# Three rows parked in device memory, the third batch made ahead of the down products, and float32 transposes, in a fused attention and feed-forward kernel

## What is computed

```python
x = x + xattn(layernorm(x), ctx, Wq, bq, Wk, bk)     # x (4, 512, 512), ctx (4, 512, 256)
x = x + ffn(layernorm(x), gate_w, up_w, down_w)      # inner width 2048

def xattn(q_rows, feat, ...):
    query, key = feat @ Wq.T + bq, feat @ Wk.T + bk
    attention = softmax(query @ key.T, axis=-1)      # (4, 512, 512)
    return einsum('bln,bmn->blm', q_rows, attention)

def ffn(x, ...):
    gate, up = mx_linear(x, gate_w), mx_linear(x, up_w)
    return mx_linear(silu(gate) * up, down_w)
# mx_linear(x, w) = mx_dequant(x) @ mx_dequant(w).T
# mx_dequant: per 32 values a scale max|v|/448, v/scale rounded to float8 e4m3, times the scale, float32
```

## Time and profile before

| | us |
|---|---|
| median of 3 runs | 609.74 |
| lowest, highest | 608.04, 609.96 |
| span of the profiled execution | 608.0 |

### The profile page before, as it was taken

How to read it: one execution, slowest core, us unless ns; L and a number is a source line. 1 busy time by engine, 2 the same in 40 slices (tenths; PEclk the granted TensorE clock), 3 DMA queues, 4 the chain that set the end, 5 groups by cost and what they waited for, 6 DMA issues and landing times.

```text
span 608.0 us, 7215 instructions
## 1 busy us (share of the span) xinstructions
PE 600.6 (99%) x2683; PEld 282.3 (46%) x2683; DVE 484.0 (80%) x455; ACT 309.2 (51%) x463; POOL 44.8 (7%) x60
## 2 busy tenths in 40 slices
PE   8999999999999999999999999999999999999998
PEld 3456554444444444444444444444444444444446
DVE  4999998899999999988999985131148899989740
ACT  3999989553555555853475532431121515254520
POOL 0000002100000001010110201000000000001100
PEclk9999999999999999999999999999999999999999
DMA  8989869989988978867445655750010334557691
GB/s 314 396 206 275 234 177 256 280 193 249 208 207 209 219 159 210 174 140 171 124 112 97 148 112 113 165 86 0 1 19 0 53 69 83 90 105 101 110 171 35
DMA packets 148162, 92.28 MB, mean 152 GB/s; under 512 B 134304, under 2 KB 134688, under 8 KB 143264
## 3 DMA queue, kind: packets, MB, share of 16 engines
q1 hardware_dynamic: 142656, 63.78, 45.2%
q0 software_dynamic: 5472, 28.05, 19.9%
HBM read 25.76 MB, written 8.39 MB: 56 GB/s over the span
## 4 chain that ended last, share of the span: by engine, by line
PE 85%; DMA 5%; issue 3%; ACT 3%; DVE 1%; SPq 1%; POOL 0%; DVEq 0%; ACTq 0%
PE bank L727 49%; PE bank L739 17%; PE bank L742 9%; PE bank L711 5%; DMA h<-in_ctxT 2%; PE bank L702 1%; PE bank L695 1%; DMA xT<-hT 1%; PE bank L687 1%; PE bank L757 1%; DMA W<-hT 1%; DMA h<-hT 1%; ACT hT L944 1%; PE bank L762 1%; ACT h L987 0%
## 5 line engine op out<-in xcount | busy, mean ns | idle before, releaser
L727 PE MATMUL bank<-gu_hi,xT 128*128 128x512 f16 x1024 | 243.6, 380 | 1.7 <-DMA xT<-hT 1.7
L727 PEld LDWEIGHTS bank<-gu_hi,xT 128*128 128x128 f16 x1024 | 99.9, 98 | 123.4 <-DMA xT<-hT 3.2
L727 PE MATMUL bank<-gu_lo,xT 128*128 128x512 f16 x512 | 131.5, 379 | 0.0
L739 PE MATMUL bank<-dn,hT 128*128 128x512 f16 x480 | 106.1, 379 | 0.0
L1633 DVE SCALAR_TENSOR_TENSOR h<-bank,unscale,silu 128x512 f32<-128x512 f32 x64 | 47.4, 747 | 56.1 <-PE bank L727 36.1
L1088 ACT ACTIVATE silu<-bank,unscale 128x512 f32<-128x512 f32 x64 | 42.8, 679 | 83.4 <-PE bank L727 40.3
L727 PEld LDWEIGHTS bank<-gu_lo,xT 128*128 128x128 f16 x512 | 50.1, 98 | 60.4
L739 PEld LDWEIGHTS bank<-dn,hT 128*128 128x128 f16 x480 | 47.0, 98 | 56.6
L1114 ACT ACTIVATE W<-h 128x2048 f16<-128x2048 f32 x16 | 30.5, 1909 | 68.3 <-DVE W L1665 25.4
L711 PE MATMUL bank<-dn,h 128*128 128x512 f32 x128 | 55.9, 593 | 0.0
L742 PE MATMUL bank<-dn,hT 128*128 128x512 f16 x240 | 54.3, 379 | 0.0
(11 more groups left out here) (119 smaller groups left out, 560.1 us busy)
## 6 DMA issues: line engine op xcount, KB each, us to landing
W<-hT POOLq DMA_DIRECT2D x12, 1024.0 KB, 5.9
W<-in_units SPq DMA_DIRECT2D x11, 1024.0 KB, 5.7
h<-W POOLq DMA_DIRECT2D x7, 1024.0 KB, 6.1
h<-in_xcols SPq DMA_DIRECT2D x4, 1024.0 KB, 12.6
out_y<-y POOLq DMA_DIRECT2D x12, 256.0 KB, 6.2
h<-in_xrows SPq DMA_DIRECT2D x2, 1024.0 KB, 11.8
out_y<-h SPq DMA_DIRECT2D x2, 1024.0 KB, 5.5
h<-hT POOLq DMA_DIRECT2D x2, 1024.0 KB, 5.9
```

The costliest lines, as they stand in the source:

```text
L727: last = pe.matmul(bank[:, :], xT[:, b % 2, part, k, :], w[:, c, g, j * 512:(j + 1) * 512], start=(j == 0 and not low), stop=(j == HT - 1 ...
L739: pe.matmul(bank[:, :], hT[:, r % 2, 0, k, :], dn[:, w, k, :], start=(k == 0 and w == 0), stop=False)
```

## The change

- `turn_probs` uses `pe.transpose` with the identity, and `weigh` scales the 128x512 row of probabilities in place by 1/sum, 16 times. The diagonals go.
- The second layernorm's rows of batch 2 are centred from SBUF (`X[2]`) into a place in the `dn` tensor that is free until the units 8 to 11 come, and not read back from `out_y`. They get their own place, so they may be made early: `n2` now comes between u7 and u8. Units 8 to 11 wait until their transposes are through.
- `h` has still 7 slots, but a table of them. Rows 4, 5 and 6, once whole, are stored to `park` in device memory (`park_row`), their slots are given to rows 7, 8 and 9, and they are read back into slots 2, 3 and 2 (`bring_row`) after the low parts of rows 2, 3 and 4 are made.
- The lists are in a new order. PE makes 44 products before `down(0)`; it was 32.
- The scratch output of `row_means` and `row_variances` is `y`, and batch 3's statistics are made later.
- All the orders (products, banks, rounds, SP, POOL, ACT, DVE) are new. The number of instructions of each kind stays, but for those named.

```diff
+    parked = (4, 5, 6)
+    slot_of = [0, 1, 2, 3, 4, 5, 6, 4, 5, 6, 0, 1, 3, 2, 4, 5]
+    slot_back = {4: 2, 5: 3, 6: 2}
+    after_parked = {7: 4, 8: 5, 9: 6}
+    after_row = {10: 0, 11: 1, 12: 5, 13: 6, 14: 7, 15: 8}
+    back_after = {4: 2, 5: 3, 6: 4}
+    park = nc.dram_tensor("park", (len(parked), P, UNIT), F32).ap()
+        third_xw = early[:, 0:UNIT]
+        third_xparts = early[:, UNIT:2 * UNIT].bitcast(F16).rearrange("p (a n) -> p a n", a=2)
...
+            def park_row(r):
+                sp.wait_ge(h_ready, max(nth[(r, c)] for c in range(CH)) + 1)
+                sp.dma_start(park_of(r), hrow(r)).then_inc(row_parked[r], 16)
+
+            def bring_row(r):
+                sp.wait_ge(row_parked[r], 16)
+                sp.wait_ge(*hidden_lo_done(back_after[r]))
+                sp.dma_start(hrow_back(r), park_of(r)).then_inc(row_back[r], 16)
...
             def turn_probs(b, nt):
                 bank = take_bank(f"t{b}.{nt}")
-                pe.wait_ge(diagonal_ready, LT * b + nt + 1)
+                pe.wait_ge(normal_ready, LT * b + nt + 1)
                 for j in range(HT):
-                    last = pe.matmul(bank[:, j * P:(j + 1) * P], probs[b][:, nt, j * P:(j + 1) * P],
-                                     diagonal[b][nt], start=(j == 0), stop=(j == HT - 1))
+                    last = pe.transpose(bank[:, j * P:(j + 1) * P], probs[b][:, nt, j * P:(j + 1) * P], idf)
                 last.then_inc(probs_turned, 1)
...
             def weigh(b, nt):
                 act.wait_ge(rsum_ready, b + 1)
-                nc.scalar.activation(diagonal[b][nt], idf, ACT.Copy, scale=rsum[:, LT * b + nt:LT * b + nt + 1]
-                                     ).then_inc(diagonal_ready, 1)
+                act.wait_ge(exp_ready, LT * b + nt + 1)
+                nc.scalar.activation(probs[b][:, nt, :], probs[b][:, nt, :], ACT.Copy,
+                                     scale=rsum[:, LT * b + nt:LT * b + nt + 1]).then_inc(normal_ready, 1)
...
             def hidden_scale(r):
+                row, s = hrow_back(r), hscale[:, r % 2, :]
+                if r in parked:
+                    dve.wait_ge(row_back[r], 16)
+                else:
+                    dve.wait_ge(h_ready, max(nth[(r, c)] for c in range(CH)) + 1)
...
-            unit_rest(0)
             unit_max(1)
             unit_max(2)
+            unit_rest(0)
             pool.wait_ge(wT_in[1], 16)
             unit_rest(1)
-            pool.wait_ge(wT_in[0], 48)
+            pool.wait_ge(wT_in[1], 32)
             unit_rest(2)
             rows_rest(0)
```

More of the change, by code:

```diff
@@ L268, in xattn_ffn @@
         odown_ready = sem("odown_ready")
+        row_parked = {r: sem(f"row{r}_parked") for r in parked}
+        row_back = {r: sem(f"row{r}_back") for r in parked}
         def unit_lo_done(u):
@@ L863, in _ @@
+            product(6, 1)
+            product(0, 2)
+            product(0, 3)
+            product(4, 2)
+            product(1, 3)
+            product(4, 3)
+            product(5, 3)
+            product(2, 3)
+            product(3, 3)
+            product(6, 3)
+            product(6, 2)
+            product(7, 1)
+            product(8, 1)
+            product(8, 3)
+            product(8, 0)
+            product(8, 2)
             product(7, 0)
-            product(7, 1)
+            product(7, 3)
@@ L1171, in _ @@
+            take_projection(3, 0)
             exponential(1, 3)
-            take_probs(0, 3)
             unit_magnitude(1)
+            exponential(2, 0)
+            row_variances(0, 1)
+            unit_rescale(1)
             weigh(1, 0)
-            take_projection(3, 0)
+            exponential(2, 1)
+            weigh(1, 1)
+            weigh(1, 2)
             unit_lo(0)
-            weigh(1, 1)
-            exponential(2, 0)
-            unit_rescale(1)
-            exponential(2, 1)
@@ new lines, in _ @@
+            silu_of(3, 2)
+            silu_of(1, 2)
+            attended_variances(2, 1)
+            unit_hi(7)
+            silu_of(4, 1)
+            rows_magnitude(2)
+            silu_of(5, 2)
+            silu_of(2, 2)
+            unit_magnitude(8)
+            unit_lo(7)
+            silu_of(6, 1)
+            silu_of(0, 2)
+            unit_rescale(8)
+            silu_of(0, 3)
+            rows_hi(2)
+            silu_of(4, 2)
+            unit_hi(8)
+            unit_lo(8)
+            silu_of(1, 3)
@@ L1282, in _ @@
+            silu_of(4, 3)
+            hidden_rescale(0)
+            unit_magnitude(9)
+            hidden_rescale(1)
+            silu_of(5, 3)
+            unit_rescale(9)
+            silu_of(2, 3)
+            silu_of(3, 3)
+            silu_of(6, 3)
+            rows_lo(2)
+            hidden_magnitude(0)
+            hidden_magnitude(1)
+            unit_hi(9)
+            silu_of(6, 2)
             unit_magnitude(10)
-            silu_of(0, 2)
-            unit_hi(9)
-            silu_of(5, 3)
@@ new lines, in _ @@
+            hidden_magnitude(5)
+            silu_of(9, 1)
+            hidden_lo(4)
+            take_down(0)
+            silu_of(10, 0)
+            hidden_rescale(5)
+            rows_hi(3)
+            silu_of(10, 1)
+            silu_of(11, 2)
+            rows_lo(3)
+            hidden_rescale(6)
+            hidden_magnitude(6)
+            hidden_hi(5)
+            silu_of(12, 3)
+            hidden_lo(5)
+            silu_of(13, 1)
+            hidden_hi(6)
+            hidden_unscale(4)
```

1009 lines of the change are left out of this document (478 added, 531 removed), and 10 rows, old and new, of the table products.

## The result

The changed kernel takes **613.79 us** (median, 613.02 to 614.27) against 609.39 for the kernel before in the same comparison (608.04 to 609.96): a ratio of **1.0066, interval 1.0049 to 1.0083**. It is slower by 4.4 us where I had forecast 4 us faster. The profiled execution has a span of 611.2 us against 608.0.

The account below looks back on a forecast made before the run. TensorE, busy 600.6 of 608.0 us, was taken as the bound, if other engines feed it earlier. 5.0 us earlier minus 1.0 of waits took 4.0 off 608.0, giving 604.0; with the 1.7 offset, 605.7 us (range 601.5 to 610.5).

Parts of the forecast that it names:

- My sign of being wrong in the first part: Attention stage: the forecast is wrong if ScalarE reaches the weighs of batch 3 later than 88 us.
- rival 4: Clock falls after TensorE idles some 5 us near 30 to 35; two slow spells cost 3.4 us: 609.1 us, chance 0.07.
- The transposes: Attention stage: one `turn_probs` falls from about 0.9 to 0.25 us, so TensorE loses 10.4 us of work over sixteen.
- ScalarE's share: Attention stage: `weigh` over the whole row costs ScalarE 0.23 us more each, 3.7 us over sixteen.
- First attend: Batch 0: ScalarE is ready at 34.4 to 34.9 us, `attend` starts there, and TensorE idles some 5 us waiting.
- the later context: Start: context 2 queues behind one more 1 MB unit; its wait ends near 20.4, not 18.45, hidden under ScalarE's wait.
- The 5.1 us at GpSimd: Before `product(3,0)`: the 5.1 us delay in issuing `rows_rest(0)` was dropped, putting the issue at 75.5 us.
- rival 2: First rows come no earlier: GpSimd's 5.1 us stays, `product(3,0)` starts at 91.6, gain 0 to 1 us: 609.3, chance 0.11.
- The later stalls: Behind `product(3,0)`: a new 1.9 us TensorE wait on silu until about 144.0, and 1.0 us charged between 250 and 300.
- Rival 5: Parking row 5 delays transposes on SyncE, then silus: 8.7 us TensorE wait at 251 to 257; 614.4 us, chance 0.15.
- Rival 3: Attention stage: transposes stay at 0.9 us each; the last four cost 2.7 us more: about 607.7 us, chance 0.05.

Follow-up runs that it names:

- f1_turns: Kernel before with only the transpose-mode `turn_probs` and `weigh` over the whole 128x512 row, no order touched: 610.50 us, ratio 1.0014.
- g3_w128: Kernel before with transposes and `rows_rest(0)` ahead of `unit_rest(2)`, but `weigh` over 128 of 512 columns, so output is not the reference's: 607.20 us.
- e4_pool: Changed kernel with `rows_rest(0)` issued ahead of `unit_rest(2)` in GpSimd's list: 610.51 us, ratio 1.0008.
- e1_silu: Changed kernel with `silu(0,0)` moved ahead of `unit_lo(3)` in ScalarE's list: 612.12 us, ratio 1.0036.
- f4_all: Changed kernel with the moves of e1_silu, e3_two and e4_pool, and `silu(2,1)` ahead of `unit_hi(4)`: 608.58 us, ratio 0.9977.
- f2_bpool: Kernel before with only `rows_rest(0)` moved ahead of `unit_rest(2)` in GpSimd's list: 608.21 us, ratio 0.9977.
- e3_two: Changed kernel with `silu(9,2)` and `silu(10,3)` ahead of batch 3's centring, and `take_down(10)` ahead of `hidden_hi(13)`: 611.70 us, ratio 1.0037.
- h2_ctxall: g4_silu11 with unit 2 loaded behind context 2 and not ahead of it: 607.54 us, ratio 0.9963.
- g4_silu11: f4_all with `silu(1,1)` also moved ahead of `unit_lo(4)` and half of batch 2's centring on ScalarE: 607.98 us, ratio 0.9972.

## Why the prediction was wrong, point by point

| step | forecast | measured |
|---|---|---|
| one `turn_probs` | 0.25 us (0.22 to 0.9) | 0.44 |
| `weigh`, each more | 0.23, 3.7 in sum | 0.30, 4.8 in sum |
| context 2 wait ends | 20.4, hidden | 21.0, not hidden |
| first attend | 34.4 to 34.9 | 35.71 |
| batch 1 attend | 55 | 55.47 |
| batch 2 attend | 72 | 72.70 |
| `rows_rest(0)` issued | 75.5 | 77.12 |
| last weigh of batch 3 ends | 86.3 | 88.8 |
| `product(3,0)` | 86.9 | 89.47 |
| waits behind it | 1.9 + 1.0 | 7.5, clock included |

The profiled span was to be 4.0 us shorter and became 3.2 longer. Of these 7.2 us, 2.6 lie ahead of `product(3,0)` (a gain of 3.1 and not 5.7) and 4.6 behind it (waits of 7.5 and not 2.9). My sign of being wrong in the first part, ScalarE at the weighs of batch 3 later than 88, did not come (86.20); the digit under 9 in the clock row, rival 4's sign, did.

**The transposes.** The value lay near the wrong row. Of the saving of 10.4 us only 7.3 is there, since a `turn_probs` takes 0.44 us. The Trainium skill, page "TensorE: Matmul & The Clock Gate", section Terms, has transpose mode four times faster for FP32. The traces here do not agree: it was two times faster, 0.44 against 0.9 us (f1_turns and the kernel before).

**ScalarE's share.** The 3.7 us were a little small (4.8), and I let the saved TensorE work stand beside them as a gain. g3_w128 shows that in the old order, where TensorE can be fed no earlier, ScalarE's term is the one that counts: there the transposes are worth nothing, +0.14% (f1_turns). In the new order it is otherwise. These are the windows from context 2 to `product(3,0)`, before and of the change:

```profile
18.60:92.60 74.00, 73.07 (x264) 40.34 (x265) 70.94 (x90) 69.24 (x158) 4.84 (x7) 1.00 0.88 250
21.00:89.40 68.40, 67.17 (x200) 32.08 (x200) 64.52 (x84) 65.22 (x133) 6.81 (x7) 1.00 0.80 222
```

TensorE is busy 67.2 of 68.4 us there, so it is its own work that fills the stage, and with the 7.3 us of the diagonals back `product(3,0)` would start near 95 (an estimate from these rows). The 3.1 us are thus the transposes and the order together. No run has the new order with the diagonals, so the share of each is not shown.

**First attend.** I let TensorE wait for ScalarE, idle some 5 us, and hid the later context under that wait. It was dense from 21.00 to 35.71, so the later context counted in full. My own terms gave that too: 20.4 and the 16.7 us of work from 18.58 to 35.24, less four times 0.65, is 34.5, the time that I gave ScalarE.

**The 5.1 us at GpSimd.** I dropped them whole. 2.3 stayed, since `unit_rest(2)` still stood ahead of `rows_rest(0)`: this is rival 2 in part. e4_pool prices it: 3.3 us of the end, since the lateness also fed the wait at `attend(3,2)`. My step took away one cause (the transpose) and did not ask what else held that queue.

**The later stalls.** This is the step that failed most: the sum charged 1.9 and 1.0 us behind `product(3,0)`, and 7.5 were there. I looked for waits near 144 and between 240 and 300. The largest was at 112, on `silu(0,0)` behind `unit_lo(3)` behind a transfer of 8.27 us, 2.62 us of wait and 1.65 of slow matmuls; the wait of 1.9 near 144 was not there at all. I wrote that "the old waits of 0.49 and 0.32 us are gone there" and walked ScalarE's list for its sum, not for what each wait in it holds up. The kind of wait that I did find, a silu behind the table loads and the unit work, comes up as soon as the earlier ones are taken away: 2.03 us in e1_silu at 131.2, and 1.03 in f4_all at 140.8, there behind `unit_lo(4)`, which waits 2.10 us for its transfer.

**Rival 4 (the clock)** had the mechanism: a lower clock behind a wait of TensorE. It had the place wrong for the profiled execution, where the fall was at 115 and not near 30. The Trainium skill, page "TensorE: Matmul & The Clock Gate", Part 1 (The HAM clock gate), states the throttling of an idle PE. The traces here agree in part: 0.69 behind a wait of 2.46 us, but none behind waits of 2.70 to 2.73 us near 20 us in six traces. One such spell costs 1.65 us in the profiled execution, near the half of rival 4's two spells. The kernel before shows almost none of it (one of 92 executions at 0.997), and no wait of TensorE behind the start is longer than 1.25 us in its own trace and that of f2_bpool.

**Rival 5 (SyncE's queue)** had nearly the measured time, 614.4, by luck and not by its cause. Its stall between 240 and 300 was 0.3 us. A wait of its kind was at 316.9: the reload of batch 3's rows, issued at 306.0 behind transposes on SyncE. It costs 1.6 us, and e3_two mends it without touching SyncE.

**Rival 3** does not follow from its own terms: 1.8 off 609.74 is 607.9 and not 607.7, and 2.7 us less gain on the forecast of 605.7 is 608.4.

**The range** of 601.5 to 610.5 left out the one rival that was slower, and with it the measured time. The sum took each place at its mean work and added almost nothing for the many new waits that a wholly new order brings. The transposes and GpSimd's issue were both set at the good side of what the rows allowed.

**The lowest median** of a kernel that computes the whole output is h2_ctxall's: 607.54, ratio 0.9963 (0.9950 to 0.9976), the changed kernel with seven lines moved; f4_all and g4_silu11 are not told from it. The kernel before with one line moved (f2_bpool) has 0.9977 (0.9964 to 0.9990); the intervals overlap, so the transposes, the parking and the new order together, once mended, have not been shown to be worth more than that one line.

## What to carry to other kernels

When a change takes work from the busiest engine, ask first which engine feeds it there. If that one is as full, count what the change adds to it, and count the saving as nothing until the order lets TensorE be fed earlier. Walk the in-order list of each feeding engine by its waits, not by its sum: each instruction that waits for a transfer holds up the bank release behind it, and a release costs nothing when it stands ahead. An idle gap of TensorE of some 2 us can cost its length and 1.7 us of slow matmuls more (2.46 and 1.65 us here), and a kernel without gaps does not show this price before a change opens one.
